# Adjacency build of a GNN kernel: one-column bank openings, stores in four paced pieces, step-innermost one-hots

## The chip, the core and the metric

The kernel runs on one core of a Trainium2 chip. The metric is the device time of one execution in microseconds (us); lower is better. The core has five engines with their own instruction queues: TensorE (PE in the profile, its weight loads PEld), VectorE (DVE), ScalarE (ACT), GpSimd (POOL) and SyncE (SP), which here issues the transfers between HBM and the on-chip memory SBUF. TensorE writes its sums into PSUM, eight banks of 512 fp32 columns for each of 128 partitions.

## The reference, cut to what matters

Four graph layers run one after the other on the same graph of 3125 nodes and 103125 edges, sorted by destination. In each the node rows are normalized, passed through the layer, and added to `x`:

```
h = relu(layernorm(x));  x = x + L0(h): segment_sum(h[src], dst) @ W_rel + h @ W_root, batch norm, relu
h = relu(layernorm(x));  x = x + L1(h): two mean-aggregating convolutions
h = relu(layernorm(x));  x = x + L2(h): attention over the edges, 8 heads
h = relu(layernorm(x));  x = x + L3(h): two relational layers, 8 edge types
```

The sums over edges of L0 and L1 are dense products with an adjacency table that the kernel first counts from `src` and `dst`. Building this table is what the change touches; everything behind it stays as it was.

## The kernel before

The table `adj` lies in HBM, 128 rows (the low 7 bits of a source) by blocks of 100 columns. A block is 4 destination nodes times 25 high parts of a source, called cells. The edges are cut into 1596 steps of up to 128 edges, each of one block, and 19 steps make an epoch (`STEPS_OF`). There are 84 epochs (`EPOCHS`), and four epochs (`GROUP`) make a window, 21 windows in all.

For an epoch `e`, VectorE compares (`compare_epochs`, L613): line 623 writes the one-hots of the low source bits, 128 by 19 fp16, and line 625 those of the cells, 19 by 100 fp16. Both have two buffers, so that VectorE waits for the steps of epoch `e - 2`.

TensorE counts (`count_edges`, L636). Line 640 loads 20 values from row 0 of SBUF into registers of its sequencer: 19 places in PSUM, one for each step, and one place in the previous window. It waits until ScalarE has emptied the half of PSUM (four banks) that epoch `e - 2` used, then opens the four banks with a matmul of zeros over 500 columns each (line 648), and runs 19 matmuls of 100 columns (line 652). In each, the one-hots of the low bits are the weights and the cells' one-hots the moving operand, and the place comes from a register. Line 657 adds the block that the previous epoch left unfinished, read back through the identity matrix, and line 661 closes the banks with one column each.

ScalarE moves each epoch's 2000 columns into one of two window buffers (`move_out`, L669; line 683), `adj_window` and `chunk_and_window`. SP (`store_windows`, L695) stores a full window of 77 blocks, 128 rows of 30,800 bytes, with one transfer (line 705), once the fourth epoch has been moved out and the previous store has landed. ScalarE may write a buffer again when the store before the last one has landed. Before the last window's store, and after the landing of the one before, SP loads the first chunk of the finished table (`load_chunk`, L710). Behind the build come seven products of such chunks with the node rows (L740). Each engine takes its instructions in the order of the code, and semaphores tie them: `ehot_n` (compared), `estep_n` (steps done), `ebuilt_n` (banks closed), `eout_n` (moved out), `s_adj` (stored).

Of the kernel before, what the change touches and what calls it, by code (L numbers as in the profile page):

```python
# [61 lines left out]
CELLS = HI * WD  # L62
KT = 7
STEPS_OF = 19
SLOTS = STEPS_OF + 1
EPOCHS = 84
MOMENTS_FROM, VARIANCE_AT, ROOT_AT, SHIFT_AT, RELU_FROM = 16, 42, 44, 48, 54
STEPS = EPOCHS * STEPS_OF
QUARTER = STEPS // 4
GROUP = 4  # L70
WINDOWS = EPOCHS // GROUP
SPANNED = GROUP * STEPS_OF + 1
CHUNK = 112
# [58 lines left out]
def build(nc, a, out):  # L132
    with ExitStack() as ctx:
        def sem(name):
            return ctx.enter_context(nc.semaphore(name))
# [26 lines left out]
        B1T = trio[:, NP:2 * NP]  # L162
# [21 lines left out]
        zeros = sb("zeros", [P, 512], F16)  # L184
# [21 lines left out]
        adj = dram("adj", [P, (KT * P + SPANNED) * CELLS])  # L206
# [21 lines left out]
        def tmp(stack, name, shape, dt=F32):  # L228
            return stack.enter_context(nc.sbuf_tensor(name, shape, dt))
# [171 lines left out]
        for q in (2, 3):  # L401
# [10 lines left out]
        carry = steprow[0:1, :, STEPS_OF:STEPS_OF + 1].rearrange("p (w g) k -> p w (g k)", g=GROUP)  # L412
        V.did(V.after().tensor_copy(carry[:, :, 1:GROUP], epochrow[0:1, :, 1:GROUP]))
        V.did(V.after().memset(carry[:, 0:1, 0:1], 0))
        stepped = V.did(V.after().tensor_tensor(carry[:, 1:WINDOWS, 0], b0w[:, 1:WINDOWS, 0], b0w[:, 0:WINDOWS - 1, 0],
                                                ALU.subtract))

        V.did(V.after(dsts).scalar_tensor_tensor(out=quarters(rels), in0=quarters(bs[:, :]), scalar=-float(WD),
                                                 in1=bank[:, 4:8, 0:QUARTER], op0=ALU.mult, op1=ALU.add))
# [177 lines left out]

        early.close()
        build = ExitStack()
        filled = [tmp(build, "adj_window", [P, SPANNED * CELLS]), arena[:, 0:SPANNED * CELLS]]  # L600
        LO, CELL = P * STEPS_OF // 2, STEPS_OF * CELLS // 2
        hot_lo = [t[:, 0:LO].bitcast(F16).rearrange("p (l k) -> p l k", k=STEPS_OF) for t in (B1T, HT)]
        hot_cell = [B1T[:, LO + j * CELL:LO + (j + 1) * CELL].bitcast(F16).rearrange("p (k c) -> p k c", c=CELLS)
                    for j in (0, 1)]
        G.need(V.now(), T.now(), A.now())
        wiped = [G.did(nc.gpsimd.memset(filled[j][:, SLOTS * CELLS * (1 - j):], 0.0)) for j in (0, 1)]
        ehot_n, estep_n, ebuilt_n, eout_n = sem("s_epoch_hots"), sem("s_epoch_steps"), sem("s_epoch_built"), sem("s_epoch_out")
        s_adj = sem("s_adj_stored")
        root_n = sem("s_first_root")
        s_held = [Dma(sem("s_chunk0")), Dma(sem("s_chunk1"))]  # L610
        held = [None, arena[:, :].rearrange("p (b h w) -> p b h w", h=HI, w=WD)]
        first_norm = {}

        def compare_epochs():
            V.after()
            for e in range(EPOCHS):
                if e == 1:
                    V.need(s_seg.now())
                if e == MOMENTS_FROM:
                    V.need(s_x.now())  # L620
                if e > 1:
                    nc.vector.wait_ge(estep_n, e - 1)
                nc.vector.tensor_tensor(hot_lo[e % 2][:, :, :], iota_lo[:, :, :],  # L623
                                        los[:, e, :].unsqueeze(1).to_broadcast([P, P, STEPS_OF]), ALU.is_equal)
                nc.vector.tensor_tensor(hot_cell[e % 2][:, :, :],
                                        iota_cell[:, :].unsqueeze(1).to_broadcast([P, STEPS_OF, CELLS]),
                                        cells[:, e, :].unsqueeze(2).to_broadcast([P, STEPS_OF, CELLS]),
                                        ALU.is_equal).then_inc(ehot_n, 1)
                if MOMENTS_FROM <= e < MOMENTS_FROM + NT:
                    tile_moments(X, [e - MOMENTS_FROM])  # L630
                if e == VARIANCE_AT:
                    first_norm["variance"] = rows_variance(0, NT)
                if e == SHIFT_AT:
                    first_norm["shift"] = rows_shift(0, NT, (root_n, 1))

        def count_edges():  # L636
            T.need(stepped, A.now())
            for e in range(EPOCHS):
                half = sums[:, (e % 2) * 2048:(e % 2 + 1) * 2048]
                place = nc.values_load_multi_w_load_instructions(  # L640
                    steprow[0:1, e, 0:SLOTS], engines=(ENG.PE,), min_val=0, max_val=(SPANNED - 1) * CELLS,
                    skip_runtime_bounds_check_because="made on the chip from counts")[1]
                place = [nc.s_assert_within(v, 0, 2048 - CELLS, skip_runtime_bounds_check_because="made on the chip")
                         for v in place[:STEPS_OF]] + [place[STEPS_OF]]
                if e > 1:
                    nc.tensor.wait_ge(eout_n, e - 1)
                for j in range(4):
                    nc.tensor.matmul(half[:, j * 512:j * 512 + SLOTS // 4 * CELLS], zeros[:, 0:P],  # L648
                                     zeros[:, 0:SLOTS // 4 * CELLS], start=True, stop=False)
                nc.tensor.wait_ge(ehot_n, e + 1)  # L650
                for k in range(STEPS_OF):
                    m = nc.tensor.matmul(half[:, bass.ds(place[k], CELLS)], hot_lo[e % 2][:, :, k], hot_cell[e % 2][:, k, :],  # L652
                                         start=False, stop=False)
                m.then_inc(estep_n, 1)
                if e:
                    nc.tensor.wait_ge(eout_n, e)
                    nc.tensor.matmul(half[:, 0:CELLS], ident[:, :],
                                     filled[(e - 1) // GROUP % 2][:, bass.ds(place[STEPS_OF], CELLS)],
                                     start=False, stop=False)
                for j in range(4):  # L660
                    m = nc.tensor.matmul(half[:, j * 512:j * 512 + 1], zeros[:, 0:P], zeros[:, 0:1], start=False, stop=True)
                m.then_inc(ebuilt_n, 1)

        def move_out():
            A.need(stepped)
            for w in range(WINDOWS):
                at = nc.values_load_multi_w_load_instructions(
                    epochrow[0:1, w, 0:GROUP], engines=(ENG.Activation,), min_val=0,
                    max_val=(SPANNED - SLOTS) * CELLS, skip_runtime_bounds_check_because="made on the chip from counts")[1]  # L669
                if w == 0:  # L670
                    nc.scalar.wait_ge(*relled)
                elif w == 1:
                    nc.scalar.wait_ge(*wiped[1])
                elif w:
                    nc.scalar.wait_ge(s_adj, 16 * (w - 1))
                for g in range(GROUP):
                    e = w * GROUP + g
                    if e == 1:
                        nc.scalar.wait_ge(*wiped[0])
                    nc.scalar.wait_ge(ebuilt_n, e + 1)  # L680
                    if e:
                        nc.scalar.wait_ge(eout_n, e)
                    nc.scalar.activation(
                        filled[w % 2][:, bass.ds(at[g], SLOTS * CELLS)].rearrange("p (a c) -> p a c", a=4),
                        bank[:, (e % 2) * 4:(e % 2) * 4 + 4, 0:SLOTS // 4 * CELLS], ACT.Copy).then_inc(eout_n, 1)
                    if e == ROOT_AT:
                        A.need(first_norm["variance"])
                        nc.scalar.activation(st["sd"][:, :], st["var"][:, :], ACT.Sqrt).then_inc(root_n, 1)
                    if e == RELU_FROM:
                        A.need(first_norm["shift"])  # L690
                    if RELU_FROM <= e < RELU_FROM + NT:
                        first_norm["rows"] = relu_tiles([e - RELU_FROM])

        def store_windows():
            nc.sync.wait_ge(*stepped)  # L695
            for w in range(WINDOWS):
                first = nc.sync.value_load(windowrow[0:1, w:w + 1], min_val=0, max_val=KT * P * CELLS)
                if w == WINDOWS - 1:
                    nc.sync.wait_ge(s_adj, 16 * w)
                    nc.sync.wait_ge(ebuilt_n, GROUP * w + 1)  # L700
                    load_chunk(0, 1)
                nc.sync.wait_ge(eout_n, GROUP * (w + 1))
                if w:
                    nc.sync.wait_ge(s_adj, 16 * w)
                nc.sync.dma_start(adj[:, bass.ds(first, SPANNED * CELLS)], filled[w % 2][:, :]).then_inc(s_adj, 16)

        def load_chunk(c, b, *marks):
            for mark in marks:
# [18 lines left out]
        nc.sync.wait_ge(s_adj, 16 * WINDOWS)  # L727
# [651 lines left out]
        for g in range(0, PAIRS, 4):  # L1379
# [5 lines left out]
            m = T.did(m)  # L1385
# [737 lines left out]
```

## Time and profile before

| | us |
|---|---|
| median of 3 runs | 3777.47 (3775.76 to 3778.92) |
| the profiled execution, its own time | 3770.99 |
| span of the profiled execution | 3769.6 |
| build of the table: first opening to last move-out | 68.25 to 485.1 |
| TensorE busy over the span | 3028.6 (80%) |
| VectorE busy over the span | 2390.8 (63%) |
| ScalarE busy over the span | 1261.2 (33%) |
| share of the 16 DMA engines of SP's queue | 35.4% of the span |

The page's busy shares are sums over the whole span, in which the build is one ninth. What bounds the build is read from views of its own stretch: the timeline of one window, the line view of single instructions and the windows view, which gives busy time, the granted TensorE clock (1.00 is 2.4 GHz, 0.50 is 1.2 GHz) and the share of time in which the DMA engines were busy.

### The profile page before, as it was taken

The page shows a single profiled execution, that of the slowest core. Times are in us where ns is not written, and L with a number is a line of the kernel's source. Part 1 is how long each engine was busy: PE and PEld are TensorE (multiplying, and loading weights), DVE is VectorE, ACT ScalarE, POOL GpSimd, SP SyncE. Part 2 cuts the span into 40 slices and gives each one's busy share as a digit, 9 for nine tenths or more (in the row PEclk, how much of TensorE's full clock was granted, in tenths as well). Part 3 has the DMA queues.
Part 4 walks back from the last instruction along what each step waited for, and adds up shares of the span by engine and source line. Part 5 has one row for each costly group of instructions (what it writes and reads, how often), then busy time and mean ns, then how long its engine had stood idle before and what let it go on. Part 6 is the DMA issues. An engine that isn't in the chain of part 4 may idle for free. (4 is left out here: it accounts for less than half of the span.)

```text
span 3769.6 us, 52194 instructions
## 1 busy us (share of the span) xinstructions
PE 3028.6 (80%) x16694; PEld 2344.0 (62%) x16694; DVE 2390.8 (63%) x3938; ACT 1261.2 (33%) x2681; POOL 1989.3 (53%) x2077
## 2 busy tenths in 40 slices
PE   5666689899688888888886479999888878787886
PEld 3555544455466666666664248888787577777775
DVE  7777768446698888888888656665555333333333
ACT  2334401100134344444433358777775200000000
POOL 4000000000277777777773157777777477777776
PEclk8788789899899999999998679999999989899987
DMA  3444475447344544444541145555555655555553
GB/s 133 182 200 210 189 322 229 187 185 291 91 114 114 116 117 114 110 117 116 117 110 43 67 149 217 202 216 195 194 201 190 233 194 195 195 195 194 195 194 93
DMA packets 236209, 633.91 MB, mean 168 GB/s; under 512 B 59204, under 2 KB 179506, under 8 KB 221088
## 3 DMA queue, kind: packets, MB, share of 16 engines
q1 hardware_dynamic: 170632, 494.18, 35.4%
q0 software_dynamic: 65312, 136.39, 14.0%
q8 instruction: 142, 2.33, 0.2%
q14 instruction: 123, 1.01, 0.1%
HBM read 412.69 MB, written 217.68 MB: 167 GB/s over the span
## 5 line engine op out<-in xcount | busy, mean ns | idle before, releaser
L1752 POOL DMA_INDIRECT edge_buffers<-rel_table,relidx x1222 | 1155.7, 946 | 459.4 <-issue 284.6
L1069 POOL DMA_INDIRECT round_buffers<-xs_t,srcs x806 | 766.2, 951 | 569.9 <-DMA xd_t<-round_buffers 324.5
L1795 PE MATMUL sums<-count_windows,H 128*128 128x208 f32 x3800 | 855.7, 362 | 30.6 <-ACT trio L1941 28.8
L1869 DVE TENSOR_TENSOR trio<-trio,sums 128x128 f32 x1242 | 356.9, 287 | 685.7 <-PE sums L1767 492.4
L1795 PEld LDWEIGHTS sums<-count_windows,H 128*128 128x128 f32 x3800 | 684.0, 203 | 47.3 <-issue 29.4
L1767 PE MATMUL sums<-edge_buffers 128*128 128x128 f32 x2340 | 372.4, 293 | 162.1 <-DMA edge_buffers<-rel_table,relidx 155.0
L1767 PEld LDWEIGHTS sums<-edge_buffers 128*128 128x128 f32 x2340 | 340.0, 202 | 190.1 <-DMA edge_buffers<-rel_table,relidx 156.1
L889 POOL IOTA trio<- 128x806 int32 x1 | 0.8, 806 | 604.0 <-ACT H L538 604.0
L1213 ACT ACTIVATE trio<-sums 128x128 f32 x806 | 223.8, 278 | 278.9 <-PE sums L1191 204.9
L1113 PE MATMUL sums<-round_buffers,ident 128*128 128x408 f32 x620 | 279.2, 534 | 30.6 <-DMA round_buffers<-xs_t,srcs 29.2
L1116 PEld LDWEIGHTS sums<-round_buffers 128*128 128x128 f32 x1612 | 243.5, 198 | 76.5 <-issue 66.1
L1933 ACT ACTIVATE count_windows<-sums 128x400 f32<-128x400 f32 x494 | 236.1, 504 | 163.6 <-PE sums L1779 157.0
L1941 ACT ACTIVATE trio<-sums 128x208 f32<-128x208 f32 x76 | 43.1, 567 | 656.4 <-PE sums L1795 642.0
L1857 DVE TENSOR_TENSOR edge_hots<-sums,edge_hots 128x4264 f16<-128x4264 f16 x76 | 180.7, 2377 | 115.7 <-ACT edge_hots L1924 115.6
L1191 PE MATMUL sums<-round_buffers 128*128 128x128 f32 x1612 | 242.8, 301 | 4.1 <-ACT trio L1213 2.1
L1116 PE MATMUL sums<-round_buffers 128*128 128x136 f32 x1612 | 244.8, 285 | 0.0
L740 PE MATMUL sums<-chunk_and_window,H 128*128 128x448 f32 x600 | 232.4, 548 | 8.4 <-DMA chunk_and_window<-adj 7.2
L1191 PEld LDWEIGHTS sums<-round_buffers 128*128 128x128 f32 x1612 | 218.0, 211 | 17.7 <-issue 14.5
L648 PE MATMUL sums<-zeros 128*128 128x500 f16 x336 | 111.0, 464 | 134.5 <-issue 126.5
L1779 PE MATMUL sums<-edge_hots 128*128 128x200 f16 x988 | 173.2, 255 | 49.7 <-DVE edge_hots L1857 46.6
L1265 DVE TENSOR_TENSOR positive<-positive,sums 128x384 f32<-128x384 f32 x310 | 152.8, 493 | 71.7 <-ACT positive L1203 71.2
L623 DVE TENSOR_TENSOR trio<-iota_lo,edge_lo 128x2432 f16<-128x2432 f16 x84 | 125.1, 1490 | 111.1 <-PE sums L652 108.7
(361 smaller groups left out, 4531.9 us busy)
## 6 DMA issues: line engine op xcount, KB each, us to landing
step_counts<-count_windows SPq DMA_DIRECT2D x38, 2600.0 KB, 9.2
count_windows<-step_counts SPq DMA_DIRECT2D x38, 2600.0 KB, 10.0
chunk_and_window<-adj SPq DMA_DIRECT2D x10, 5600.0 KB, 16.1
round_buffers<-xd_t SPq DMA_DIRECT2D x806, 68.0 KB
adj_chunk<-adj SPq DMA_DIRECT2D x9, 5600.0 KB, 16.6
adj<-adj_window SPq DMA_DIRECT2D x11, 3850.0 KB, 11.5
adj<-chunk_and_window SPq DMA_DIRECT2D x10, 3850.0 KB, 10.9
rel_table<-table_stages SPq DMA_DIRECT2D x50, 512.0 KB, 2.6
```

Source lines behind the costliest of these rows:

```text
L740: m = nc.tensor.matmul(ps.rearrange("p (b w) -> p b w", w=WD), tables[:, hi, :], held[b][:, :, hi, :], start=(hi == 0), stop=(hi == HI - 1))
L1069: nc.gpsimd.indirect_dma_start(rows[r % RING][:, k * RW:(k + 1) * RW], None, xs_t[:, :], bass.IndirectOffsetOnAxis(ap=srcs[:, t:t + 1], ax ...
L1113: nc.tensor.matmul(pb[2 + q % 2][:, 0:(hi - lo) * RW], ident[:, :], rows[r % RING][:, lo * RW:hi * RW], start=True, stop=False)
L1116: m = nc.tensor.matmul(pb[2 + q % 2][:, (k - lo) * RW:(k - lo + 1) * RW], hotT[r % 2][:, k * P:(k + 1) * P], win[r % 2][:, k * RW:(k + 1) ...
L1191: m = nc.tensor.matmul(pb[6 + q % 2][:, (k - lo) * P:(k - lo + 1) * P], msg[:, k * P:(k + 1) * P], hot[r % 2][:, k * P:(k + 1) * P], start ...
L1213: nc.scalar.activation(pairs[:, bass.ds(at[k], P)], pb[6 + q % 2][:, (k - lo) * P:(k - lo + 1) * P], ACT.Copy).then_inc(out_n, 1)
L1752: nc.gpsimd.indirect_dma_start(slot(p * IG + i, k), None, rel_t[p][:, :], bass.IndirectOffsetOnAxis(ap=relidx[:, i * U + k:i * U + k + 1], ...
L1767: nc.tensor.matmul(part_of(g)[:, (k - lo) * P:(k - lo + 1) * P], slot(q, k), round_hots(q)[:, k, :], start=True, stop=True).then_inc(summe ...
L1795: m = nc.tensor.matmul(pb[4][:, 0:SW * R].rearrange("p (s r) -> p s r", r=R), H[:, h, :], counts[:, w % 2, :, h * R:(h + 1) * R], start=(h ...
L1857: nc.vector.tensor_tensor(ehot[:, half], numbers.unsqueeze(1).to_broadcast([P, RUN, P + HR]), ehot[:, half], ALU.is_equal).then_inc(onehot ...
L1869: nc.vector.tensor_tensor(held, held, part_of(g)[:, j * P:(j + 1) * P], ALU.add).then_inc(added_n, 1)
L1933: nc.scalar.activation(counts[:, w % 2, 2 * j:2 * j + 2, :].rearrange("p s c -> p (s c)"), pb[q % 3][:, 0:2 * HR], ACT.Copy).then_inc(evic ...
```

## The change

Three edits, all inside the build:

- From the third epoch on, the four banks of a half are opened by a matmul of one column each (column 511) in place of 500. A block that no step of an epoch touches then keeps old data. So the cell one-hots, the register of the carried block and the window buffers are adapted: where an epoch begins with a new block, the carried place is that of a block of zeros appended to each window buffer (`SPANNED * CELLS`), worked out by three more one-row VectorE operations.
- The store of a window is issued as four transfers of 32 partitions each (`PIECES_OF`), and piece `g` of window `w` waits for `eload_n`, which TensorE raises with the openings of epoch `4 (w + 1) + g`, behind that epoch's register load. The last two windows have no such wait. The waits on `s_adj` count four landings for each window.
- The cells' one-hots are laid out as 100 cells by 19 steps, the step innermost, compared against a constant of the same shape that ScalarE makes once (line 612 of the changed kernel). TensorE reads its 100 moving columns at a stride of 19 elements, as it reads its weights before and after.

SP's queue, between two windows in the middle of the build, before (`ISA` rows are register work, `windowrow` holds the place in HBM):

```order
L697 TENSOR_LOAD windowrow
L697 ISA x2
L705 REGISTER_ALU [waits s_adj_stored,s_epoch_out]
L705 DMA adj<-chunk_and_window 128x7700
L697 TENSOR_LOAD windowrow
L697 ISA x2
```

and the same place now:

```order
L713 TENSOR_LOAD windowrow
L713 ISA x2
L725 REGISTER_ALU [waits s_epoch_loaded,s_adj_stored,s_epoch_out]
L725 DMA adj<-chunk_and_window 32x7700
L725 ISA [waits s_epoch_loaded]
L725 DMA adj<-chunk_and_window 32x7700
L725 ISA [waits s_epoch_loaded]
L725 DMA adj<-chunk_and_window 32x7700
L725 ISA [waits s_epoch_loaded]
L725 DMA adj<-chunk_and_window 32x7700
```

One transfer became four, and each of the four stands behind a wait for TensorE's openings.

TensorE's queue, from the end of one epoch to the first step of the next (epochs 2 and 3), before:

```order
L661 MATMUL sums<-zeros 128x1 x4
L640 TENSOR_LOAD steprow
L648 MATMUL sums<-zeros 128x500 [waits s_epoch_out]
L648 MATMUL sums<-zeros 128x500 x3
L652 ISA [waits s_epoch_hots]
L652 MATMUL sums<-trio 128x100
```

and now:

```order
L676 MATMUL sums<-zeros 128x1 x4
L649 TENSOR_LOAD steprow
L658 MATMUL sums<-zeros 128x1 [waits s_epoch_out]
L658 MATMUL sums<-zeros 128x1 x3
L663 ISA [waits s_epoch_hots]
L663 MATMUL sums<-trio 128x100
```

No instruction moved or went; the openings shrank from 500 columns to one.

The diff, cut to its core:

```diff
@@ tables of the build @@
+        V.did(V.after().tensor_tensor(b0[:, 1:EPOCHS], bs0[:, 1:EPOCHS, 0], bs0[:, 0:EPOCHS - 1, STEPS_OF - 1], ALU.is_equal))
+        begun = steprow[0:1, 1:EPOCHS, STEPS_OF]
+        V.did(V.after().scalar_tensor_tensor(out=begun, in0=begun, scalar=float(SPANNED * CELLS), in1=b0[:, 1:EPOCHS],
+                                             op0=ALU.subtract, op1=ALU.mult))
+        stepped = V.did(V.after().tensor_scalar(begun, begun, float(SPANNED * CELLS), None, ALU.add))
...
-        filled = [tmp(build, "adj_window", [P, SPANNED * CELLS]), arena[:, 0:SPANNED * CELLS]]
+        filled = [tmp(build, "adj_window", [P, (SPANNED + 1) * CELLS]), arena[:, 0:(SPANNED + 1) * CELLS]]
-        hot_cell = [B1T[:, LO + j * CELL:LO + (j + 1) * CELL].bitcast(F16).rearrange("p (k c) -> p k c", c=CELLS)
+        hot_cell = [B1T[:, LO + j * CELL:LO + (j + 1) * CELL].bitcast(F16).rearrange("p (c k) -> p c k", k=STEPS_OF)
+        iota_cells = tmp(build, "iota_cells", [P, CELLS, STEPS_OF], F16)
+        A.need(V.now(), T.now())
+        celled_out = A.did(A.after().activation(iota_cells[:, :, :],
+                                                iota_cell[:, :].unsqueeze(2).to_broadcast([P, CELLS, STEPS_OF]), ACT.Copy))
@@ compare_epochs @@
-            V.after()
+            V.after(celled_out)
                 nc.vector.tensor_tensor(hot_cell[e % 2][:, :, :],
-                                        iota_cell[:, :].unsqueeze(1).to_broadcast([P, STEPS_OF, CELLS]),
-                                        cells[:, e, :].unsqueeze(2).to_broadcast([P, STEPS_OF, CELLS]),
+                                        iota_cells[:, :, :],
+                                        cells[:, e, :].unsqueeze(1).to_broadcast([P, CELLS, STEPS_OF]),
@@ count_edges @@
                 for j in range(4):
-                    nc.tensor.matmul(half[:, j * 512:j * 512 + SLOTS // 4 * CELLS], zeros[:, 0:P],
-                                     zeros[:, 0:SLOTS // 4 * CELLS], start=True, stop=False)
+                    first = 0 if e < 2 else 511
+                    m = nc.tensor.matmul(half[:, j * 512 + first:(j + 1) * 512], zeros[:, 0:P], zeros[:, first:512],
+                                         start=True, stop=False)
+                m.then_inc(eload_n, 1)
                 for k in range(STEPS_OF):
-                    m = nc.tensor.matmul(half[:, bass.ds(place[k], CELLS)], hot_lo[e % 2][:, :, k], hot_cell[e % 2][:, k, :],
+                    m = nc.tensor.matmul(half[:, bass.ds(place[k], CELLS)], hot_lo[e % 2][:, :, k], hot_cell[e % 2][:, :, k],
+                if e == 1:
+                    nc.tensor.wait_ge(*wiped[0])
+                if e == GROUP + 1:
+                    nc.tensor.wait_ge(*wiped[1])
@@ store_windows @@
-                    nc.sync.wait_ge(s_adj, 16 * w)
-                nc.sync.dma_start(adj[:, bass.ds(first, SPANNED * CELLS)], filled[w % 2][:, :]).then_inc(s_adj, 16)
+                    nc.sync.wait_ge(s_adj, 16 * PIECES_OF * w)
+                n = P // PIECES_OF
+                for g in range(PIECES_OF):
+                    if w < WINDOWS - 2:
+                        nc.sync.wait_ge(eload_n, GROUP * (w + 1) + g + 1)
+                    nc.sync.dma_start(adj[g * n:(g + 1) * n, bass.ds(first, SPANNED * CELLS)],
+                                      filled[w % 2][g * n:(g + 1) * n, 0:SPANNED * CELLS]).then_inc(s_adj, 16)
```

## Rows read from the trace of the kernel before

**Rows 1.** SP timeline, 305 to 326 us: start, us, engine, line, operation

```profile
305.13 0.33 SPq L705 DMA_DIRECT2D adj<-chunk_and_window  x1
325.12 0.33 SPq L705 DMA_DIRECT2D adj<-adj_window  x1
```

**Rows 2.** line view, TensorE's register load L640: all, then windows 97:103, 305:318, 477:481

```profile
L640 PEldq TENSOR_LOAD <-steprow x84: 1356/1376/4807, 64.8 to 478.5; - x84
...
L640 PEldq TENSOR_LOAD <-steprow x2: 1357/1360/1362, 98.5 to 102.6; - x2
...
L640 PEldq TENSOR_LOAD <-steprow x2: 2467/3386/4306, 306.4 to 313.4; - x2
...
L640 PEldq TENSOR_LOAD <-steprow x1: 1372/1372/1372, 478.5 to 478.5; - x1
```

**Rows 3.** TensorE timeline, 303 to 311 us, with the idle time before each

```profile
303.93 1.00 PE L648 MATMUL sums<-zeros 128*128 128x500 f16 x4 [0.90 <-issue]
304.76 1.74 PE L652 MATMUL sums<-trio 128*128 128x100 f16 x19
306.36 0.46 PE L657 MATMUL sums<-chunk_and_window,ident 128*128 x2
310.74 1.82 PE L648 MATMUL sums<-zeros 128*128 128x500 f16 x4 [3.85 <-issue]
```

**Rows 4.** line views of L652 and L648 in 303:307: sequencer and weight loads

```profile
L652 PEldq FUSED_REGOPS  x19: 37/37/42, 303.9 to 306.2; - x19
L652 PEld LDWEIGHTS sums<-trio x19: 135/144/158, 304.6 to 306.2; 128*128 128x128 f16 x19
...
L648 PEld LDWEIGHTS sums<-zeros x4: 95/96/96, 303.9 to 304.3; 128*128 128x128 f16 x4
```

**Rows 5.** windows: busy by engine, granted clock, share of DMA engines busy, GB/s

```profile
core 0: us, PE busy (x) PEld busy (x) DVE busy (x) ACT busy (x) POOL busy (x), PEclk, DMA share, GB/s
305.00:325.00 20.00, 12.77 (x120) 10.02 (x119) 14.70 (x9) 7.35 (x4) 0.00 (x0) 0.91 0.47 198
307.00:314.00 7.00, 3.26 (x25) 2.23 (x26) 3.27 (x2) 1.84 (x1) 0.00 (x0) 0.76 0.99 422
477.50:494.00 16.50, 8.69 (x80) 7.40 (x78) 3.99 (x8) 3.68 (x2) 0.00 (x0) 0.81 0.98 383
```

**Rows 6.** line view of the stores, L705: time from issue to landing

```profile
DMA to landing us min/median/max: 10.6/11.3/19.2
```

**Rows 7.** windows, as above: around a load into eight partitions

```profile
2033.60:2035.10 1.50, 1.33 (x9) 1.14 (x10) 0.00 (x0) 1.07 (x4) 0.00 (x0) 0.94 0.30 69
```

**Rows 8.** DMA view: data packets of 2033.6:2035.1, and the issue's size (2032.5:2037)

```profile
DMA packets 16, 0.10 MB, mean 69 GB/s; under 512 B 8, under 2 KB 8, under 8 KB 8
...
round_buffers<-piece_t SPq DMA_DIRECT2D x1, 100.8 KB
```

**Rows 9.** lines view, 150:700: both comparisons and the evictions

```profile
L625 DVE TENSOR_TENSOR trio<-iota_cell,edge_cell 128x1900 f16<-128x1900 f16 x66 | 140.6, 2130 | 0.0
L623 DVE TENSOR_TENSOR trio<-iota_lo,edge_lo 128x2432 f16<-128x2432 f16 x65 | 96.9, 1490 | 90.6 <-PE sums L652 90.4
L683 ACT ACTIVATE adj_window<-sums 128x2000 f32 x35 | 64.3, 1838 | 106.9 <-PE sums L661 106.9
```

**Rows 10.** timeline: ScalarE's L315, TensorE's first opening, SP at the build's end

```profile
4.75 2.23 ACT L315 ACTIVATE iota_lo<-iota 128x2432 f16<-128x2432 f32 x1
...
68.25 1.82 PE L648 MATMUL sums<-zeros 128*128 128x500 f16 x4 [4.39 <-issue]
...
476.47 0.35 SPq L710 DMA_DIRECT2D chunk_and_window<-adj  x1
485.28 0.34 SPq L705 DMA_DIRECT2D adj<-adj_window  x1
504.48 0.34 SPq L710 DMA_DIRECT2D adj_chunk<-adj  x1
```

**Rows 11.** TensorE timeline, 515 to 523 us

```profile
520.40 2.87 PE L740 MATMUL sums<-adj_chunk,H 128*128 128x448 f32 x5 [2.33 <-DMA adj_chunk<-adj]
```

More of the change, by code:

```diff
@@ L70 @@
 GROUP = 4
+PIECES_OF = 4
 WINDOWS = EPOCHS // GROUP
@@ L414, in build @@
         V.did(V.after().memset(carry[:, 0:1, 0:1], 0))
-        stepped = V.did(V.after().tensor_tensor(carry[:, 1:WINDOWS, 0], b0w[:, 1:WINDOWS, 0], b0w[:, 0:WINDOWS - 1, 0],
-                                                ALU.subtract))
+        V.did(V.after().tensor_tensor(carry[:, 1:WINDOWS, 0], b0w[:, 1:WINDOWS, 0], b0w[:, 0:WINDOWS - 1, 0], ALU.subtract))
+        V.did(V.after().tensor_tensor(b0[:, 1:EPOCHS], bs0[:, 1:EPOCHS, 0], bs0[:, 0:EPOCHS - 1, STEPS_OF - 1], ALU.is_equal))
[3 more added lines that the diff above has]
+        stepped = V.did(V.after().tensor_scalar(begun, begun, float(SPANNED * CELLS), None, ALU.add))
         V.did(V.after(dsts).scalar_tensor_tensor(out=quarters(rels), in0=quarters(bs[:, :]), scalar=-float(WD),
@@ L608, in build @@
         s_adj = sem("s_adj_stored")
-        root_n = sem("s_first_root")
+        root_n, eload_n = sem("s_first_root"), sem("s_epoch_loaded")
         s_held = [Dma(sem("s_chunk0")), Dma(sem("s_chunk1"))]
@@ L640, in count_edges @@
                 place = nc.values_load_multi_w_load_instructions(
-                    steprow[0:1, e, 0:SLOTS], engines=(ENG.PE,), min_val=0, max_val=(SPANNED - 1) * CELLS,
+                    steprow[0:1, e, 0:SLOTS], engines=(ENG.PE,), min_val=0, max_val=SPANNED * CELLS,
                     skip_runtime_bounds_check_because="made on the chip from counts")[1]
@@ L660, in count_edges @@
                 for j in range(4):
-                    m = nc.tensor.matmul(half[:, j * 512:j * 512 + 1], zeros[:, 0:P], zeros[:, 0:1], start=False, stop=True)
+                    m = nc.tensor.matmul(half[:, j * 512 + 511:j * 512 + 512], zeros[:, 0:P], zeros[:, 0:1],
+                                         start=False, stop=True)
                 m.then_inc(ebuilt_n, 1)
@@ L674, in move_out @@
                 elif w:
-                    nc.scalar.wait_ge(s_adj, 16 * (w - 1))
+                    nc.scalar.wait_ge(s_adj, 16 * PIECES_OF * (w - 1))
                 for g in range(GROUP):
@@ L703, in store_windows @@
                 if w:
-                    nc.sync.wait_ge(s_adj, 16 * w)
-                nc.sync.dma_start(adj[:, bass.ds(first, SPANNED * CELLS)], filled[w % 2][:, :]).then_inc(s_adj, 16)
+                    nc.sync.wait_ge(s_adj, 16 * PIECES_OF * w)
+                n = P // PIECES_OF
[4 more added lines that the diff above has]
+                                      filled[w % 2][g * n:(g + 1) * n, 0:SPANNED * CELLS]).then_inc(s_adj, 16)
         def load_chunk(c, b, *marks):
@@ L726, in build @@
         dsum = B1T[:, NP - DST:NP].rearrange("p (b w) -> p b w", w=WD)
-        nc.sync.wait_ge(s_adj, 16 * WINDOWS)
+        nc.sync.wait_ge(s_adj, 16 * PIECES_OF * WINDOWS)
         nc.sync.wait_ge(eout_n, EPOCHS)
```

## The prediction

> **What bounds the kernel now.** I read the windows view of one window of the build, then TensorE's timeline in it, then the line view of its register load, and last the DMA side. A window of four epochs takes 20.0 us: its stores are issued at 305.13 and 325.12 [rows 1]. No engine is full in that time: TensorE is busy for 12.77 of 20 us, VectorE for 14.70, ScalarE for 7.35, and the DMA engines for 47% [rows 5]. So the chain is one of waits. TensorE's timeline shows it: after the closing of an epoch it is idle for 0.90 us "issue", and once in a window for 3.85 us [rows 3]. What runs there is the load of 20 registers by its sequencer, 1.36 us when nothing is in flight, but 4.31 and 2.47 us for the two that fall into a store [rows 2]. The load that starts at 478.5 takes 1.37 us although the first chunk comes in at 98% busy DMA engines around it [rows 2, 5]. So it is reads of SBUF by a store that slow the load, to 1.36 / 4.31 = 0.32 of its speed, and not writes into it.
>
> The rest of an epoch is dispatch. From the end of the load that starts at 302.5 (303.87) to the start of the next (306.38, read as 306.4) pass 2.5 us, in which the sequencer issues 19 times a register operation, a weight load and a matmul [rows 2, 4]. Over the window it is (20.0 - 2 x 1.36 - 4.31 - 2.47) / 4 = 2.63 us an epoch. The array is faster: the openings occupy 303.93 to 304.76, and the 19 steps have caught up with the dispatch when they end at about 306.4 [rows 3]. So per window: 4 x 2.63 of dispatch, 2 x 1.36 of undisturbed loads, 6.8 of slowed ones, sum 20.0.
>
> **One-column openings: nothing.** They take about 0.8 us of array time from each of 82 epochs. The steps behind them can't start to be dispatched earlier, since the sequencer issues the same instructions in the same order and the first dispatch already lies beside the openings. Above, the gain is bounded by 82 x 0.8 = 66 us, if the array were the bound; below by 0. I take 0, since the gap from load to load holds 19 dispatches at about 0.12 us each and the array ends with them. The new waits for the two memsets on POOL stand behind the steps of epochs 1 and 5; ScalarE waits for the same memsets now.
>
> **New layout: nothing.** VectorE's comparison of the cells has the shape of the other one now, so 1900 columns take about 1.49 x 1900 / 2432 = 1.16 us in place of 2.13 [rows 9]. It saves 84 x 0.97 = 81 us of VectorE, whose own chain (3.6 us an epoch) is shorter than TensorE's four and waits for it 90.6 us in sum [rows 9]. The gain is covered by TensorE. The constant costs ScalarE about 2.23 x 1900 / 2432 = 1.7 us at 65 us, and the first comparison slides from 62.7 to about 66.5; both comparisons are done by 69.2, before the first step, which follows openings that end at 70.0 [rows 10]. The three one-row operations of VectorE fall into its wait for TensorE before the build.
>
> TensorE's strided reading has no row as a moving operand. Below it costs 0. Above, the nearest row is the weight load at the same stride, 144 ns for four parts of 32 columns, against 96 for a contiguous one: 48 ns more for 32 reads, so 150 for 100 [rows 4]. A step of the array, 0.09 us in the timeline (1.74 / 19), would be 0.24 and 19 steps 4.6 us, 1.3 us over the epoch of 4.0. I take 0, since a step may grow by a third before it passes the dispatch. The Trainium skill ("SBUF — State Buffer", Door 1: The DMA port swizzle) says that consecutive accesses run at full rate only within a line of 16 bytes, and here every element lies in a line of its own; by that rule the step grows, by how much the page doesn't say, and no row shows it.
>
> **Four paced stores: slower.** The store moves 3.94 MB at 422 GB/s while it runs, with 99% of the DMA engines busy [rows 5], so 9.35 us; issue to landing is 11.3 [rows 6], so 1.95 us lie around it. Each engine then moves 26.6 GB/s. A piece has 32 partitions, two rows of 30.8 KB for each engine. If engines keep their rate, it takes 2.34 us. But partitions seem to have a limit of their own. The only row of a transfer into few partitions is a load of 100.8 KB into eight of them: its eight data packets keep 30% of 16 engines busy for 1.5 us, 7.2 engine-us, so 14.3 GB/s for each [rows 7, 8], a little over half of 26.6. With that rate a piece takes 61.6 / 14.3 = 4.3 us. So the bounds are 2.34 and 4.3 to 4.7 (half rate). I take 4.5, since the row shows engines that share few partitions at half speed, and 32 is a quarter of 128. By the same section of the Trainium skill, 32 partitions reach 8 of 16 ports and one MiB moves at 189 GB/s; an estimate from that page is 5.2 us a piece, and the sum would be 30 to 50 us longer than mine.
>
> At 4.5 us the DMA engines need 18.0 us for a window, and with the 1.9 us around them (the first piece waits for the landing of all before) 19.9. That alone would be 20 us again. The pacing adds to it. A piece's data starts about 1.2 us after the end of its epoch's load (0.35 for openings and wait, 0.85 from issue to data) and ends at 5.7; the next load begins at 2.63. So it overlaps for 3.1 us, gets 0.98 us of its work done at 0.32 of its speed, and takes 3.1 + 0.38 = 3.5 us; at half that speed, with two engines at the partition's door, 4.0. The registers come from partition 0, so I count this for the two pieces of the lower 64 partitions and not for the upper two. TensorE's window is 4 x 2.63 + 2 x 1.36 + 2 x 3.6 = 20.4, with some waiting of the two chains for each other 20.5. Over 18 paced windows: +9 us.
>
> The last two stores aren't paced, and they stand in a row: landing, chunk load at 476.47, last store at 485.28 behind it on the DMA engines, chunk load at 504.48 [rows 10], for which TensorE waits at 520.40 [rows 11]. Each grows from 9.35 to 18.0: +17 us.
>
> Sum: +26 us on the profiled execution's own 3771.0, so 3797. The median of the runs shown lies 6.5 above that execution, so the forecast as a median is 3803.
>
> **Rivals.** (a) The pieces keep the full rate, 2.34 us. A piece ends 3.5 us after the load; the next load overlaps 0.9 us and takes 2.0, the one behind the first piece, which waits for the move-out some 1.1 us longer, 2.7. TensorE's window is 10.5 + 3 x 2.0 + 2.7 = 19.2 if all pieces slow it, 17.9 if only the lower two do: 19 windows x 0.8 to 2.1 = 16 to 40 us less. As the first piece is also held less in a shorter window I put it at 35 less: 3742. For it speaks that eight partitions are not 32. 22 in 100. (b) Full rate and no load is met: 10.5 + 4 x 1.36 = 15.9, so 4.1 x 19.5 = 80 less, 3697. Against it, the 1.2 us of delay. 5 in 100. (c) The new store chain of 19.9 us is the bound and the tail is partly covered by chunk work: within 7 us, 3777. 12 in 100. (d) The upper pieces slow the loads too, since the trace doesn't tell whether the slowing belongs to partition 0 or to all reads: 10.5 + 4 x 3.6 = 24.9, +4.9 x 18 and the tail: up to 3877, at half the slowing 3830. 7 in 100. (e) The strided matmul bounds the array at 5.3 us an epoch from 0.2 us a step on: 21.2 a window, +22 and +17: 3816. 4 in 100.
>
> **Numbers.** The forecast has 50 in 100 with its own range of 3782 to 3825 (pieces of 4.3 to 4.7, slowed loads of 3.3 to 4.2). A measurement of this kernel can tell a change from none at about 0.2%, 7.5 us. Faster: (a) and (b), 27. Same: (c), 12. Slower: 61. The range of 3728 to 3850 leaves out (b) and the far part of (d).
>
> **What would show it.** The DMA view has 84 pieces of 962.5 KB: by their landing, about 6.5 us undisturbed against 4.3, the forecast stands or falls, and with it the DMA share of a window, still 47% at full rate and about 90% at half. Register loads of TensorE: two of four near 3.6 us. The openings' idle time stays "issue"; windows take 20.5 us; the last store lands about 19 us after its data begins. VectorE's second comparison at 1.16 us with longer waits confirms the cover. If windows are at 18 us or less, (a) is right and my reading of the eight partitions wrong.

## The result and the profile after

| | before | after |
|---|---|---|
| median, us | 3778.18 (3775.76 to 3778.92, 4 runs) | 3902.57 (3900.44 to 3905.58, 4 runs) |
| ratio | | 1.0331, 95% interval 1.0313 to 1.0349 |
| span of the profiled execution, us | 3769.6 | 3899.1 |
| granted clock, mean over the span | 0.897 | 0.851 |

The change costs 124 us. The forecast was +26 (3803, range to 3850): the sign was right, and the size was off by a factor of nearly five. The windows view of one window of the changed kernel, and of the stretch of one piece in it:

```profile
core 0: us, PE busy (x) PEld busy (x) DVE busy (x) ACT busy (x) POOL busy (x), PEclk, DMA share, GB/s
300.00:325.60 25.60, 17.16 (x117) 14.04 (x116) 11.71 (x16) 7.35 (x4) 0.00 (x0) 0.50 0.74 154
305.60:310.60 5.00, 3.12 (x21) 2.46 (x19) 2.34 (x2) 1.76 (x1) 0.00 (x0) 0.50 0.95 197
```

A window takes 25.6 us where it took 20.0 [rows 5]. The DMA engines are busy for twice as long (74% of 25.6 us against 47% of 20.0): in the stretch of a piece they are as busy as before, 0.95 against 0.99, but move 197 GB/s against 422. TensorE's granted clock is 0.50 throughout.

The line view of TensorE's register load (now L649), with shortest, median and longest in ns: all, the four of that window, and the two that lie under an unpaced store:

```profile
L649 PEldq TENSOR_LOAD <-steprow x84: 1357/3711/6344, 65.6 to 592.3; - x84
...
L649 PEldq TENSOR_LOAD <-steprow x4: 3571/3720/4127, 300.6 to 319.3; - x4
...
L649 PEldq TENSOR_LOAD <-steprow x2: 5233/5788/6344, 575.5 to 584.6; - x2
```

The median over the build rose from 1376 to 3711 ns [rows 2]. In a window no load is fast any more: all four take 3.6 to 4.1 us, where two took 1.36. TensorE's timeline of one epoch shows the hole that this leaves, and what the array does in the rest:

```profile
304.42 0.24 PE L658 MATMUL sums<-zeros 128*128 128x1 f16 x4 [2.22 <-ACT chunk_and_window L699]
304.54 3.68 PE L663 MATMUL sums<-trio 128*128 128x100 f16 x19
308.04 0.60 PE L672 MATMUL sums<-chunk_and_window,ident 128*128 x2
308.43 0.29 PE L676 MATMUL sums<-zeros 128*128 128x1 f16 x4
310.67 0.25 PE L658 MATMUL sums<-zeros 128*128 128x1 f16 x4 [1.95 <-ACT chunk_and_window L699]
```

The idle time before the openings is put down to ScalarE, whose move-out TensorE also waits for; but the load that starts at 306.9 lasts 3.71 us, and the openings come 0.06 us behind its end. The openings shrank from 1.00 to 0.24 us, the 19 steps grew from 1.74 to 3.68 [rows 3]. Their sum stays below the 6.3 us of an epoch.

The stores in the line view of L725:

```profile
DMA to landing us min/median/max: 6.1/6.1/23.5
```

In the DMA view, with transfer, count, size and median landing:

```profile
adj<-adj_window SPq DMA_DIRECT2D x44, 962.5 KB, 6.1
```

And in SP's timeline, in the window and at the build's end (a row of several issues runs from the start of the first to the end of the last):

```profile
304.83 6.57 SPq L725 DMA_DIRECT2D adj<-adj_window  x2
317.38 6.83 SPq L725 DMA_DIRECT2D adj<-chunk_and_window  x2
...
573.58 5.61 SPq L725 DMA_DIRECT2D adj<-chunk_and_window  x4
593.69 0.38 SPq L731 DMA_DIRECT2D chunk_and_window<-adj  x1
600.70 1.87 SPq L725 DMA_DIRECT2D adj<-adj_window  x4
625.69 0.37 SPq L731 DMA_DIRECT2D adj_chunk<-adj  x1
```

A piece is a quarter of a store and lands after 6.1 us, more than half of the 11.3 that the whole one took [rows 6]. In the window of 300 us the data packets of one piece run from 305.64 to 310.58, 4.94 us. The engine that begins last needs 4.73 us of them (from 305.85) for its 61.6 KB, 13.0 GB/s where the whole store has 26.6. So pieces read at half rate. From the next-to-last store's issue to the second chunk load pass 52.1 us, where it was 38.7 (465.77 to 504.48). TensorE's first product of the other chunk buffer starts here [rows 11]:

```profile
642.67 3.83 PE L761 MATMUL sums<-adj_chunk,H 128*128 128x448 f32 x5 [7.12 <-DMA adj_chunk<-adj]
```

This gives the account of the 129.5 us between the two spans. The next-to-last store is issued 107.8 us later than before (573.58 against 465.77), which is 18 windows of 5.6 and 7 at their two ends. TensorE's product starts 122.3 us later (642.67 against 520.40), so the tail adds 14.5. The last 7 come behind the build; most of them can be scatter, since the profiled execution of before lay 7.2 us under its median and that of the change 2.1.

### The profile page after: what moved, and what is told of

Same layout as the page of the kernel before. It is cut to its first block and busy times, and to the rows that moved or that the text cites. A ratio compares the mean times of both kernels' runs of the same rounds, so it can differ in the third digit from the quotient of the medians.

```text
span 3899.1 us, 52392 instructions
## 1 busy us (share of the span) xinstructions
PE 3112.5 (80%) x16694; PEld 2423.1 (62%) x16694; DVE 2316.4 (59%) x3941; ACT 1264.5 (32%) x2682; POOL 1992.9 (51%) x2077
## 5 line engine op out<-in xcount | busy, mean ns | idle before, releaser
L1816 PEld LDWEIGHTS sums<-count_windows,H 128*128 128x128 f32 x3800 | 682.0, 203 | 47.1 <-issue 29.2
L663 PE MATMUL sums<-trio 128*128 128x100 f16 x1596 | 308.3, 363 | 0.1
L663 PEld LDWEIGHTS sums<-trio 128*128 128x128 f16 x1596 | 220.4, 140 | 56.7 <-issue 1.1
L1212 PEld LDWEIGHTS sums<-round_buffers 128*128 128x128 f32 x1612 | 217.6, 210 | 17.3 <-issue 14.5
```

Source lines behind the costliest of these rows:

```text
L1212: m = nc.tensor.matmul(pb[6 + q % 2][:, (k - lo) * P:(k - lo + 1) * P], msg[:, k * P:(k + 1) * P], hot[r % 2][:, k * P:(k + 1) * P], start ...
L1816: m = nc.tensor.matmul(pb[4][:, 0:SW * R].rearrange("p (s r) -> p s r", r=R), H[:, h, :], counts[:, w % 2, :, h * R:(h + 1) * R], start=(h ...
```

## The experiments

Twelve kernels, in three groups; each group shared its runs of the kernel before. The first two groups ran on other chips, on which the kernel before takes 4680 us. The changed kernel's trace from there has a span of 4801.4 us against 3899.1; its windows of the build are the same to 0.1 us, and the difference lies behind the build. So for those runs ratios and the rows of the build are what counts.

**One part at a time.** The pieces alone, on the kernel before:

```diff
-                nc.sync.dma_start(adj[:, bass.ds(first, SPANNED * CELLS)], filled[w % 2][:, :])...
+                for g in range(PIECES_OF):
+                    if w < WINDOWS - 2:
+                        nc.sync.wait_ge(eload_n, GROUP * (w + 1) + g + 1)
+                    nc.sync.dma_start(adj[g * n:(g + 1) * n, bass.ds(first, SPANNED * CELLS)], ...
```

> The kernel before with one part of the change: the window's store in four pieces of 32 partitions, paced by the next epochs' loads; openings of 475 columns and the old layout stay. Theory 1 (the pieces): each is read out of SBUF at half rate, so one is in flight at every register load, and all four loads of a window take 3.7 us instead of 4.3, 2.5, 1.4 and 1.4. Then this kernel has nearly all of the loss: a window of 25.5 us, the last two stores 13 us later together, 3885 to 3905 us. Theory 2 (the strided read and the cold clock make TensorE's array or its sequencer the bound): the window stays at 20 to 21 us and the time at 3778 to 3800 us. Theory 3 (openings of one column starve the clock, and the clock costs the time): as theory 2, 3778 to 3795 us.

The ratio is 1.0399 (1.035 to 1.0448), +187 us on 4680: all of the loss, and more. The openings and the layout alone, with a whole store:

```diff
-                for g in range(PIECES_OF): ... (four pieces, paced)
+                nc.sync.dma_start(adj[:, bass.ds(first, SPANNED * CELLS)],
+                                  filled[w % 2][:, 0:SPANNED * CELLS]).then_inc(s_adj, 16)
```

> The changed kernel with its store in one whole transfer, as before the change: openings of one column and the new layout alone. Theory 1: register loads go back to 4.3, 2.5, 1.4 and 1.4 us, the window to 20.0 us, and the time to 3770 to 3790 us, although the strided read still takes 190 ns a step at a granted clock of 0.50. Theories 2 and 3: the window stays near 25 us and the time above 3850 us.

Ratio 1.001 (0.9984 to 1.0036): nothing. First the pieces alone: the register loads of one window in the line view, with the first of the next.

```profile
L641 PEldq TENSOR_LOAD <-steprow x5: 4137/4559/5030, 370.6 to 399.9; - x5
```

The same window in the windows view:

```profile
370.60:400.00 29.40, 15.66 (x123) 11.32 (x121) 14.57 (x10) 8.86 (x6) 0.00 (x0) 0.67 0.70 145
```

Then the kernel with the whole store, the loads of one window in the line view:

```profile
L649 PEldq TENSOR_LOAD <-steprow x4: 1361/1790/4433, 295.0 to 310.0; - x4
```

Its windows view:

```profile
290.10:310.00 19.90, 16.74 (x118) 13.75 (x116) 10.77 (x11) 8.86 (x6) 0.00 (x0) 0.50 0.47 199
```

With the whole store two loads in four are near 1.36 again and the window is 19.9 us, at a clock of 0.50 and with TensorE busy for 16.74 us of it. So neither the strided read nor the cold clock made the loss. What theory 1 had not foreseen is that the pieces alone are worse than the whole change, 29.4 us a window (29.2 in the mean of the build) against 25.6. The changed kernel once more, and the changed kernel without its layout:

> The changed kernel once more, beside the kernel before on whatever chip this is: the chip of the first four runs took 4680 us for the kernel before, 900 us more than the first one, so what counts is the difference to the kernel before and the window of the build. All theories: window 25.6 us and 115 to 130 us over the kernel before.

> The changed kernel with the layout of before, so that only openings of one column and the paced pieces are left. The pieces alone had a window of 28.9 us and loads of 4.6 us, worse than the whole change with 25.6 and 3.7. Theory A: the openings of 475 columns end later than those of one column, and with them the go-ahead of each piece, so more of its 4.9 us lies over the next load; then this kernel equals the whole change: window 25.6 us, loads 3.7 us, same time within 10 us. Theory B: the layout is what helps (VectorE done sooner); then the window is 28 us or more and the time 40 us or more above the changed kernel.

```diff
-    iota_cells[:, :, :], cells[:, e, :].unsqueeze(1).to_broadcast([P, CELLS, STEPS_OF])
+    iota_cell[:, :].unsqueeze(1).to_broadcast([P, STEPS_OF, CELLS]), cells[:, e, :].unsqueeze(2)...
...
-                    ... hot_cell[e % 2][:, :, k]
+                    ... hot_cell[e % 2][:, k, :]
```

Ratios 1.0248 (1.0201 to 1.0295) and 1.0207 (1.0167 to 1.0247). The loads in the line view, first of the changed kernel, over the build:

```profile
L649 PEldq TENSOR_LOAD <-steprow x84: 1357/3715/6337, 66.4 to 593.4; - x84
```

Then without the layout, in one window:

```profile
L645 PEldq TENSOR_LOAD <-steprow x4: 3628/3709/4120, 316.8 to 336.3; - x4
```

Theory A holds: without the layout the loads stay at 3.7 us, and the windows are 25.6 us in the mean in both. The two medians lie 13 us apart, a little more than the 10 of theory A, but the executions of one kernel scatter by up to 27 us there, so a difference isn't shown. What the change gains over the pieces alone comes from the openings, which carry the go-ahead of a piece. TensorE's timeline of the pieces alone shows it:

```profile
367.97 1.83 PE L649 MATMUL sums<-zeros 128*128 128x500 f16 x4 [2.93 <-ACT adj_window L685]
...
376.71 1.79 PE L654 MATMUL sums<-trio 128*128 128x100 f16 x19
```

SP's timeline of the same kernel, at the first of these openings:

```profile
369.98 0.32 SPq L711 DMA_DIRECT2D adj<-chunk_and_window  x1
```

Openings of 500 columns (the expectations say 475) at a clock of 0.50 take 1.83 us, and the piece is issued 2.0 us after they begin (369.98 against 367.97). In the changed kernel it is 0.4 us (304.83 against 304.42). The later piece lies over more of the next load.

**What halves the rate, and what the pacing does.** Pieces of 1925 columns over all partitions, and pieces of every fourth partition:

```diff
-    adj[g * n:(g + 1) * n, bass.ds(first, SPANNED * CELLS)], filled[w % 2][g * n:(g + 1) * n, ...]
+    adj[:, bass.ds(first + g * 1925, 1925)],  filled[w % 2][:, g * 1925:(g + 1) * 1925]        # columns
+    adj[g:P:4, bass.ds(first, SPANNED * CELLS)], filled[w % 2][g:P:4, 0:SPANNED * CELLS]        # every fourth
```

> The changed kernel with four pieces of 1925 columns over all 128 partitions in place of 32 partitions with all columns; pacing, openings and layout as in the change. Theory 1 with the half rate as its cause: a piece lasts 2.3 to 2.7 us instead of 4.9, so of its data only the last us or so lies over the next register load, which takes 1.9 to 2.4 us; window 4 x 2.1 + 10.5 = 18 to 19.5 us, and 3740 to 3775 us in all. Rival (the pacing or the number of transfers costs it, whatever their shape): all four loads stay at 3.5 us or more, window above 24 us, time above 3860 us.

> The changed kernel with each piece of 32 partitions taken as every fourth partition instead of 32 that lie together; packets, bytes, pacing as in the change. Theory 1a (the half rate comes from reading neighbouring partitions only): a piece lasts 2.4 to 2.7 us, register loads 1.8 to 2.9 us as with pieces of columns, window 19.2 us, at most 10 us off the kernel before. Theory 1b (the half rate comes from few, long packets, two for each engine): pieces stay at 4.9 us, loads at 3.7 us, window 25.6 us, 115 to 130 us over the kernel before.

Ratios 0.9997 (0.9972 to 1.0021) and 0.9994 (0.9972 to 1.0015): the whole loss is gone in both. The pieces of columns, their landing in the line view of the stores:

```profile
DMA to landing us min/median/max: 3.7/3.7/16.5
```

The loads of one of their windows:

```profile
L649 PEldq TENSOR_LOAD <-steprow x4: 1701/1970/2912, 288.4 to 303.0; - x4
```

Every fourth partition, the pieces in the DMA view:

```profile
adj<-adj_window SPq DMA_DIRECT2D x44, 962.5 KB, 4.0
```

The loads of one of their windows:

```profile
L649 PEldq TENSOR_LOAD <-steprow x4: 2073/2270/2797, 274.8 to 290.1; - x4
```

The second one decides between 1a and 1b. Its packets are those of the change, 32 of 30,800 bytes, two for each engine; only the partitions they come from differ. A packet takes 1.17 us instead of 2.38, as in the whole store before (1.16, means over the packets of the build). So it is the neighbouring partitions that halve the rate, and theory 1b falls. The Trainium skill ("SBUF — State Buffer", Door 1: The DMA port swizzle) has the rule: partitions 0 to 31 reach 8 of the 16 ports, and the partition number's bits 2 to 4 and 6 pick the port, so that every fourth partition reaches all of them. Its 189 GB/s for 32 partitions is near the 986 KB in 4.94 us, 200 GB/s, of a piece of neighbours, and both runs agree with the rule.

The gain over the kernel before was to be 3 to 38 us for the columns, and isn't there to be seen: the windows are 19.0 us in the mean, 0.9 less than before, and 18 of them are 17 us, while the interval spans 23.

The same 32 partitions without pacing, on the kernel before:

```diff
-                    if w < WINDOWS - 2:
-                        nc.sync.wait_ge(eload_n, GROUP * (w + 1) + g + 1)
```

> The kernel before with the store in four pieces of 32 partitions that are all issued at once, without pacing. Theory 1: the four pieces follow one another at half rate, 20 to 24 us of data in a window, so that all loads are slowed just as with pacing: window 25 us or a little over, 3880 to 3920 us. Rival (pacing costs it: the data is spread over loads that were free): issued at once the pieces go together at the rate of the whole store, two loads in four are free again, window 20 to 21 us, time under 3800 us.

Ratio 1.0261 (1.0214 to 1.0308), +122 us. One window in the windows view:

```profile
356.40:382.60 26.20, 14.85 (x122) 11.11 (x120) 14.57 (x10) 7.35 (x4) 0.00 (x0) 0.70 0.76 162
```

Its four loads:

```profile
L641 PEldq TENSOR_LOAD <-steprow x4: 1361/4003/6233, 356.4 to 374.8; - x4
```

The pieces follow one another, as theory 1 says, and the window is 26.2 us (25.5 in the mean), so it isn't the pacing that costs. But "all loads slowed" was wrong: one in four stays at 1.36 us. Two lie wholly in the data and take longer than under a whole store (4.3), and not the same: the one under the first two pieces, partitions 0 to 63, takes 6.2 us, the one under the last two 5.2. It is so in nearly all windows, 6.1 to 6.4 against 5.2 to 5.3. Since the pieces always go in this order, the trace can't tell whether the partitions or the order make the difference.

**Pacing that misses the loads.** If a load is slowed by data in flight and by nothing else, a short piece should be let go so that its data falls between two loads. Pieces of columns, let go by the end of an epoch's steps (`estep_n`), in three kernels: with all edits, on the kernel before, and with openings of one column and the old layout:

```diff
-                        nc.sync.wait_ge(eload_n, GROUP * (w + 1) + g + 1)
+                        nc.sync.wait_ge(estep_n, GROUP * (w + 1) + g + 1)
```

> The changed kernel with pieces of 1925 columns over all partitions, each let go when the last step of an epoch is done, which is when the next register load begins, and not at the opening. Theory 1 (a load is slowed for as long as a store's data moves, at 0.3 to 0.4 of its speed, and by nothing else): the data starts 1.2 us after the go-ahead and lasts 2.4 us, so it lies over the end of nothing but the opening and the steps; loads of 1.4 to 1.6 us, window 4 x 1.5 + 10.5 = 16.5 us, 60 to 70 us under the kernel before. Rival (a load is slowed by transfers being issued or by any store that is near it): loads above 2 us, window 18.5 us or more, and no more than 30 us under the kernel before.

> The kernel before with one thing new: its store in four pieces of 1925 columns over all partitions, each let go when the steps of an epoch are done; openings of 475 columns and the old layout stay. Theory 1: the pieces' data now lies between the loads, loads of 1.4 to 1.6 us, window 16.5 to 17 us, 45 to 70 us under the kernel before, the same as with the openings and the layout of the change. Rival (the shorter openings and the layout carry part of that gain, since at 4.1 us an epoch TensorE's array has little left over): window above 17.5 us, at least 15 us slower than the last version with all edits.

> The same pieces with openings of one column and the old layout (steps read at 2 bytes' distance). Theory 1: window 16.5 to 17 us, within 10 us of the other two versions of this kind. Rival: with 190 ns a step at a clock of 0.50 the strided read had become part of the bound (3.9 of 4.2 us an epoch); then this one, at 83 ns a step, is the fastest, with a window near 16.3 us and at least 10 us less.

Ratios 0.9844 (0.9798 to 0.9891), 0.9838 (0.9821 to 0.9854) and 0.9835 (0.9818 to 0.9851). The last two ran on a chip with the times of the first, 3711.96 and 3711.28 us beside 3773.03: 61 us under the kernel before, and about 190 under the change. With all edits, the four loads of a window in the line view:

```profile
L649 PEldq TENSOR_LOAD <-steprow x4: 1416/1505/1827, 248.6 to 261.4; - x4
```

And that window in the windows view:

```profile
248.56:265.31 16.75, 16.61 (x117) 13.82 (x116) 10.42 (x8) 8.87 (x6) 0.00 (x0) 0.50 0.56 231
```

On the kernel before, loads and window:

```profile
L641 PEldq TENSOR_LOAD <-steprow x4: 1357/1421/1564, 248.4 to 260.5; - x4
```

The windows view:

```profile
248.40:264.90 16.50, 13.52 (x119) 10.66 (x118) 14.48 (x10) 8.87 (x6) 0.00 (x0) 0.79 0.59 241
```

With openings of one column and the old layout, loads and window:

```profile
L645 PEldq TENSOR_LOAD <-steprow x4: 1362/1458/1460, 248.0 to 260.1; - x4
```

The windows view:

```profile
248.00:264.40 16.40, 13.62 (x119) 12.79 (x117) 14.57 (x10) 8.86 (x6) 0.00 (x0) 0.50 0.59 243
```

Theory 1 gets its loads of 1.4 to 1.6 us and its window of 16.5. The whole gain comes from the kernel before with the new store alone; openings and layout add nothing. With all edits TensorE's array is busy for 16.61 of 16.75 us: the strided read has used up its slack, though it doesn't bind yet, since from the end of a load to the next pass 2.64 us as before. That kernel's gain, 73 us by its ratio (51 to 95 by its interval), or 51 by the medians' difference, is too wide to be told from the other two.

**Openings and layout apart**, with a whole store and one execution each (before: 3773.03 us):

> The kernel before with openings of one column alone (whole store, old layout). Forecast of the prediction: a step 83 ns at a clock of 0.50, granted clock 0.50 throughout the build, register loads of 4.3, 2.5, 1.4 and 1.4 us or the same sum, window 20.0 us: no gain and no loss. Rival: the cold clock costs the build; window above 20.5 us.

> The kernel before with the new layout alone (whole store; openings of whole banks of 512 columns). The strided read costs the array something for each column: 190 ns against 83 ns for a step at 0.50. If it is a fixed number of the array's clocks a column, a step takes 95 to 115 ns where the clock is 1.00 and the sequencer hides it (2.65 us for 19 steps, 140 ns each). If it is a time of the memory that does not go with the clock, a step stays at 190 ns. In both cases VectorE's comparison takes 1.2 us and the window stays at 20.0 us.

```diff
-                    first = 0 if e < 2 else 511
+                    first = 0                                  # layout only
```

The openings alone took 3781.2 us, with 1374 ns as the median of the loads and a granted clock of 0.50: nothing, or a loss of up to 8 us that a single run can't settle. In its trace a window is 20.2 us in the mean against 20.0, all of it in the two loads under the store. The layout alone took 3852.05 us, 79 us more than before, and the expectation of 20.0 us a window was plainly wrong. Its windows view, with one whole window and a stretch at each clock:

```profile
320.40:343.80 23.40, 21.59 (x118) 14.79 (x117) 10.42 (x8) 8.86 (x6) 0.00 (x0) 0.72 0.40 169
306.20:309.50 3.30, 3.30 (x20) 2.55 (x19) 0.59 (x1) 0.40 (x1) 0.00 (x0) 0.50 0.71 299
329.40:332.60 3.20, 3.20 (x19) 2.49 (x18) 1.66 (x2) 1.25 (x1) 0.00 (x0) 1.00 0.36 154
```

Its TensorE timeline:

```profile
304.51 1.87 PE L658 MATMUL sums<-zeros 128*128 128x512 f16 x4
306.17 3.65 PE L663 MATMUL sums<-trio 128*128 128x100 f16 x19
...
329.41 3.64 PE L663 MATMUL sums<-trio 128*128 128x100 f16 x19
```

At a clock of 0.50 an epoch fills the array for 5.8 us (its openings begin at 304.51, its closing at 310.03 ends at 310.3), more than the 4.0 us of load and dispatch. The array is the bound there: from the end of a load to the next pass 3.59 us in the mean. Steps start every (3.65 - 0.36) / 18 = 0.183 us at a clock of 0.50 and every (3.64 - 0.36) / 18 = 0.182 at 1.00. The old layout in the timeline of the pieces alone, also at 0.50, is at (1.79 - 0.29) / 18 = 0.083. So the strided read costs 0.10 us a step over the old one at a clock of 0.50, and its pace did not follow the clock. The short openings are what hid it in the changed kernel: they gave back 1.6 us of the 1.9 that the read took.

## Why the prediction was right or wrong

- **What bounds the build**: right. Sequencer time, register loads and dispatch, is the chain, and reads of SBUF by a store slow a load. From the end of a load to the start of the next pass 2.63 to 2.65 us in the mean in every kernel except the layout alone, with granted clocks from 0.50 to a mean of 0.89, and only the loads differ. The three kernels with the new pacing bring the window to 16.4 to 16.8 us, near 4 x (1.36 + 2.63) = 16.0.
- **Openings, 0**: right in sum. But they had two effects that I didn't list: they made the array's slack that the new layout then took, and they moved the go-ahead of the pieces forward by 1.6 us (25.6 against 29.4 us a window).
- **Layout, 0**: right for VectorE (1.19 us measured, 1.16 said). For TensorE the 0 came out, but not for my reason. I let a step grow by a third before it passes the dispatch, with a bound of 0.24 us a step; it more than doubled, from 0.083 to 0.183 us, which passes the dispatch, 2.63 / 19 = 0.14 us. It costs nothing in the changed kernel because the steps run on beneath the next load and the short openings make room for them; that it met these openings was luck, and in the layout alone it cost 79 us. The rule of the Trainium skill that I had set against it ("SBUF — State Buffer", Door 1: The DMA port swizzle, the 16-byte line) had the right sign.
- **Pieces, 4.5 us each from the eight-partition load**: the size was right, 4.73 us for one engine's share and 4.94 for the piece. The reason, few partitions, was too wide: 32 partitions that are every fourth one read at the full rate. This term decided the sign, and rivals (a) and (b) fell with it.
- **The step that failed**: "The registers come from partition 0, so I count this for the two pieces of the lower 64 partitions and not for the upper two." All four pieces slow a load, to 3.57 to 4.13 us, those of partitions 64 to 127 to 3.71 and 3.57 in the window shown. The trace of before showed slowing by a whole store only and couldn't say which partitions did it; I gave my story 50 chances in 100 and its rival (d) only 7. I had worked (d) out at 3877, from the profiled execution's 3771; from the median, as the other rivals, it is 3883. Two loads of 3.7 in place of 1.36 are 4.7 of the 5.1 us a window that I missed; over 18 windows 5.1 is 92 us. Rival (d)'s window was 24.9 us, measured 25.6.
- **Tail, +17**: 14.5 measured, right in the main. From issue to landing the next-to-last store grew by 9.4 us (20.1 for 10.7). The last one lands 13.0 us behind the first chunk in place of 9.1, so it grew by 3.9 only and not by the 8.65 of the sum: part of its data already moves beside the chunk's. The second chunk load takes 1.1 longer.
- 26 of the sum, 92 of the failed step, 7 at the two ends of the paced windows and 7 behind the build, less 2.5 of the tail, make the 129.5 us between the two spans. Between the medians it is 124.
- **The range**: 3728 to 3850 left out what (d) gives at its full size. Its near end was inside, its far end wasn't.

What stays open: why a load in the changed kernel ends together with a piece's data (310.61 and 310.58) after 3.7 us, while one that lies wholly in such data needs 6.3, or 5.2 under the two upper pieces. That load lies under the third piece; by a constant ratio of 1.36 / 5.23 = 0.26 it should have taken 4.1. And which resource a load and a store share was not isolated. Shown is that stores of partitions 64 to 127 slow a load too; whether those of the lower half slow it more, as 6.3 against 5.2 us suggest, is open.

## What to carry to other kernels

Before a transfer is cut up, look at which partitions a piece reads: cut by columns, or take every n-th partition, and not a block of 32 neighbours, which read at half rate here. Where a sequencer loads registers from SBUF in its critical chain, look at which transfers out of SBUF are in flight then, and pace short pieces to fall between the loads. And where a trace can't tell whether a cost belongs to a part or to the whole, price both and let the chance follow what is known, not the neater story.

## What the runs showed of the hardware

- A load of 20 registers takes 1.36 us undisturbed, 4.3 wholly under a store that reads at full rate, and 5.2 to 6.3 wholly under pieces of 32 neighbouring partitions that follow one another at half rate: the slower transfer slows it more. It ran undisturbed, 1.37 us, beside a load from HBM into SBUF at 98% busy DMA engines.
- An fp16 moving operand of 100 columns, each 38 bytes from the next, takes 0.183 us at a granted clock of 0.50 and 0.182 at 1.00, 1.8 ns a column; contiguous it takes 0.083 us at 0.50.
- The granted clock of the build was 0.50 with openings of one column and 0.80 in the mean in the kernel before, and where the sequencer is the bound that cost nothing: with the new pacing 3711.28 us at 0.50 and 3711.96 at a mean of 0.79 in the window.
